# One transformer block in one launch: the shift of the attention's maximum on ScalarE, all lower parts of the probabilities on GpSimd, relative scores by one load, rotary sums out of the PSUM bank

## What is computed

```python
def _L0_attn_ref(x, w_q, w_k, w_v, w_o, rel_emb):        # 16 heads of 8 features
    q = _apply_rotary_interleave(shape(x @ w_q.T), cos, sin) / sqrt(DIM_PER_HEAD)
    k = _apply_rotary_interleave(shape(x @ w_k.T), cos, sin)
    scores = jnp.einsum('bhqd,bhkd->bhqk', q, k)
    rel = rel_emb[clip(pos_k - pos_q, -32, 32) + 32]
    scores = scores + jnp.einsum('bhqd,qkd->bhqk', q, rel)
    attn = softmax(where(causal, scores, NEG_INF))
    ctx = jnp.einsum('bhqk,bhkd->bhqd', attn, v) + jnp.einsum('bhqk,qkd->bhqd', attn, rel)
    return ctx.transpose(0, 2, 1, 3).reshape(B, L, MODEL_DIM) @ w_o.T
...
for wg, wu, wd in experts:                                # 8 experts, 128 -> 512 -> 128
    acc = acc + (silu(x @ wg) * (x @ wu)) @ wd
...
x = x + 0.5 * ffn(layernorm(x))
x = x + attn(layernorm(x))
x = x + 0.5 * ffn(layernorm(x))
```

## Time and profile before

| | before |
|---|---|
| median of 3 runs | 1345.06 us (1344.24 to 1345.31) |
| the profiled execution | 1341.76 us, of which the span from first to last instruction is 1340.0 us |
| PE busy | 1314.1 us, 98% |
| DVE busy | 1220.2 us, 91% |
| POOL busy | 1068.3 us, 80% |
| ACT busy | 1048.7 us, 78% |
| attention's first and last `scores` | 133.7 us and 1236.1 us |

### The profile page before, as it was taken

How to read it: one execution, slowest core, us unless ns; L and a number is a source line. 1 busy time by engine, 2 the same in 40 slices (tenths; PEclk the granted TensorE clock), 3 DMA queues, 4 the chain that set the end, 5 groups by cost and what they waited for, 6 DMA issues and landing times. The chain is left out here.

```text
span 1340.0 us, 28494 instructions
## 1 busy us (share of the span) xinstructions
PE 1314.1 (98%) x8334; PEld 1052.6 (79%) x8334; DVE 1220.2 (91%) x2609; ACT 1048.7 (78%) x2098; POOL 1068.3 (80%) x980
## 2 busy tenths in 40 slices
PE   8999999999999999999999999999999999999798
PEld 6888877777788777778887778777887788888586
DVE  6887989999999999999999999999999999999565
ACT  6765878888878888788888888878888888888354
POOL 6986978889787878798778878788877887878465
PEclk9999999999999999999999999999999999999899
DMA  6504799999899999999989999999999999998300
GB/s 188 162 1 132 139 183 203 185 205 206 179 201 174 196 176 182 207 183 197 188 158 221 184 189 181 173 234 170 192 183 164 226 188 178 180 193 144 60 1 8
DMA packets 719517, 225.02 MB, mean 168 GB/s; under 512 B 653441, under 2 KB 698881, under 8 KB 719361
## 3 DMA queue, kind: packets, MB, share of 16 engines
q1 hardware_dynamic: 562224, 180.84, 69.1%
q10 hardware_dynamic: 157136, 42.36, 17.5%
HBM read 60.95 MB, written 69.86 MB: 98 GB/s over the span
## 5 line engine op out<-in xcount | busy, mean ns | idle before, releaser
L1219 POOL TENSOR_TENSOR hid_lo<-hid,hid_hi 128x512 fp32r<-128x512 f32 x512 | 663.4, 1304 | 170.9 <-ACT hid_hi L927 125.9
L921 ACT ACTIVATE hid<-work 128x512 f32<-128x512 f32 x512 | 305.8, 602 | 112.7 <-PE work L788 96.0
L1053 DVE SCALAR_TENSOR_TENSOR hid<-hid,work 128x512 f32<-128x512 f32 x512 | 343.1, 678 | 46.3 <-ACT hid L921 45.8
L1059 DVE TENSOR_TENSOR hid<-hid,work 128x512 f32<-128x512 f32 x512 | 345.6, 679 | 24.1 <-PE work L727 21.7
L927 ACT CAST hid_hi<-hid 128x512 fp32r<-128x512 f32 x512 | 318.8, 627 | 60.5 <-DVE hid L1059 36.7
L1234 POOL TENSOR_TENSOR probs<-exps,probs 128x512 f16<-128x512 f32 (+1 forms) x288 | 305.1, 1064 | 65.7 <-ACT probs L979 64.0
L968 ACT ACTIVATE exps<-work,negmax_shifted 128x512 f32<-128x512 f32 (+2 forms) x320 | 188.4, 605 | 46.0 <-DVE negmax_shifted L1159 27.3
L1153 DVE TENSOR_REDUCE negmax<-work 128x1 f32<-128x384 f32 (+3 forms) x352 | 219.9, 631 | 0.9
L784 PE MATMUL work<-xt,wg 128*128 128x512 f32 x512 | 205.6, 402 | 4.0 <-DVE hid L1053 2.5
L725 PE MATMUL work<-xt,wu 128*128 128x512 f32 x512 | 204.5, 399 | 0.5 <-ACT g_s L955 0.2
L808 PE MATMUL acc<-hid_lo,wd 128*128 128x512 f32 x512 | 203.4, 400 | 1.1 <-POOL hid_lo L1219 0.9
(11 more groups left out here) (94 smaller groups left out, 1745.6 us busy)
## 6 DMA issues: line engine op xcount, KB each, us to landing
prob_window_scratch<-probs SPq DMA_DIRECT2D x384, 80.0 KB, 2.9
rel_win<-rel_window_scratch ACTq DMA_DIRECT2D x250, 96.0 KB, 3.6
q_scratch<-rope SPq DMA_DIRECT2D x16, 512.0 KB, 4.6
qq<-q_scratch ACTq DMA_DIRECT2D x32, 256.0 KB, 3.5
k_scratch<-rope SPq DMA_DIRECT2D x16, 512.0 KB, 4.2
rel_window_scratch<-g_s SPq DMA_DIRECT2D x32, 256.0 KB, 3.8
k_pad<-k_scratch SPq DMA_DIRECT2D x128, 64.0 KB, 3.6
prob_window_scratch<-probs SPq DMA_DIRECT2D x32, 256.0 KB, 3.8
```

The lines of the kernel that those rows point to most:

```text
L921: act.activation(hid[:, arg % HB, :], work[bank_of["gate", arg]][:, :], ACT.Tanh, scale=0.5).then_inc(s_tanh, 1)
L1053: dve.scalar_tensor_tensor(out=hid[:, arg % HB, :], in0=hid[:, arg % HB, :], scalar=1.0, in1=work[bank_of["gate", arg]][:, :], op0=ALU.add ...
L1059: dve.tensor_tensor(hid[:, arg % HB, :], hid[:, arg % HB, :], work[bank_of["up", arg]][:, :], ALU.mult).then_inc(s_hid, 1)
L1219: pool.tensor_tensor(hid_lo[:, arg % HH, :], hid[:, arg % HB, :], hid_hi[:, arg % HH, :].bitcast(F32), ALU.subtract).then_inc(s_hlo, 1)
```

## The change

- `lent` is gone: all 352 tasks put their exponentials into `exps` (two buffers), all lower parts are made by POOL, and the bank of a task is free after `exp`. DVE makes no lower part of probabilities.
- `shift` is one ACT instruction for a task (1, 2 or 4 columns), with the bias in a small constant tile; DVE makes none. 
- `load_window` is one DMA of 128 rows by 160 columns (320 KB) where it was two of 64 rows by 96 columns (96 KB each), on ACT's queue.
- The product with the sines goes back into the PSUM bank it came from, and the sum reads it there.
- `ln_scaled` signals each of its four tiles, and PE transposes each as it comes.
- At the very end, the last `lo` (chunk 511) is DVE's, and `acc`, `sum_turned`, `sum` and `store` of the last pass are done in two halves.
- The planner's costs follow, and every number of `LATER` is another, and so is the whole order.

```diff
-    LATER = {"acc": -1001.3, "attention_sum": -224.3, "band_turn": -664.1, "band_values": -890.3, "constants":
...
+    LATER = {"acc": -1204.3, "attention_sum": 8.3, "band_turn": -791.5, "band_values": -878.0, "constants":
...
-        step("POOL", 1.25, at + 3.7, "lo", n, ("hi", n), ("down_lo", back(n, HH)))
+        step("POOL" if n < NP * CH - 1 else "DVE", 1.25 if n < NP * CH - 1 else wide(L), at + 3.7, "lo", n, ("hi", n), ("down_lo", back(n, HH)))
...
-            step("DVE", wide(L) + w % 2 * 0.9, at, "rotate", (t, w), ("project", (t, w)))
+            step("DVE", wide(L) * (1 + w % 2), at, "rotate", (t, w), ("project", (t, w)))
...
-                step("ACT", 1.03, max(begin - 13, first - 13), "load_window", quad, ("qrel_store", gg),
+                step("ACT", 0.42, max(begin - 13, first - 13), "load_window", quad, ("qrel_store", gg),
...
-                 ("load_k", quad // NT), done_with(back(k, 2)))
+                 ("load_k", quad // NT), ("exp", back(k, 2)))
-            if lent(k):
-                step("DVE", 0.07 * HEADS[i], due[k] + 0.8, "shift", k, ("largest", k))
-            step("ACT", HEADS[i] * 0.07 + columns / 1200, due[k] + 1, "exp", k, ("shift" if lent(k) else "largest", k),
-                 ("p_lent", lent_before(k, EB) if lent(k) else None))
-            step("ACT", act_wide(columns) + 0.04 * lent(k), due[k] + 1.5, "p_hi", k, ("exp", k), ("store_band", back(k, PB)),
+            step("ACT", 0.15, due[k] + 0.8, "shift", k, ("largest", k))
+            step("ACT", HEADS[i] * 0.07 + columns / 1200, due[k] + 1, "exp", k, ("shift", k), ("p_lo", back(k, EB)))
+            step("ACT", act_wide(columns) + 0.04, due[k] + 1.5, "p_hi", k, ("exp", k), ("store_band", back(k, PB)),
                  ("p_turn", back(k, PB)))
-            if lent(k):
-                step("POOL", 0.04 + columns / 475, due[k] + 2, "p_lent", k, ("p_hi", k))
-            else:
-                step("DVE", wide(columns), due[k] + 2, "p_lo", k, ("p_hi", k))
+            step("POOL", 0.04 + columns / 475, due[k] + 2, "p_lo", k, ("p_hi", k))
...
+    spare = next(b for b in range(BANKS) if tenant[b][0] in ("gate", "up"))
...
-                    sp.wait_ge(s_sum, PASS_OF["B", arg] + 1)
-                    sp.dma_start(out_v[arg], x_s[arg % XB][:, :].rearrange("p (t d) -> p t d", t=NT)
-                                 ).then_inc(s_out[arg % XB], 16)
+                    x = x_s[arg % XB][:, :].rearrange("p (t d) -> p t d", t=NT)
+                    halves = (slice(0, NT),) if arg < B - 1 else (slice(0, NT // 2), slice(NT // 2, NT))
+                    for h, half in enumerate(halves):
+                        sp.wait_ge(s_sum, PASS_OF["B", arg] + 1 + h)
+                        sp.dma_start(out_v[arg][:, half, :], x[:, half, :]).then_inc(s_out[arg % XB], 16)
...
+            def norm_turned(m, bank):
+                for i in range(NT):
+                    pe.wait_ge(s_xn, NT * m + i + 1)
+                    done = pe.transpose(bank[:, i * P:(i + 1) * P], xn[:, i * P:(i + 1) * P], ident[:, :])
+                done.then_inc(s_xnt, 1)
...
-                    if was == "scores" and not lent(x):
-                        pe.wait_ge(*lower_part(x))
-                    if was == "scores" and lent(x):
+                    if was == "scores":
                         quad, i, places, _ = task(x)
                         pe.wait_ge(s_exp, unit(quad, places[-1]) + 1)
...
-                    pe.wait_ge(s_acc, arg + 1)
-                    transposes(bank, acc_t).then_inc(s_ftok, 1)
+                    if arg < NP - 1:
+                        pe.wait_ge(s_acc, arg + 1)
+                        transposes(bank, acc_t).then_inc(s_ftok, 1)
+                    else:
+                        pe.wait_ge(s_hid, NP * CH)
+                        for i in range(NT):
+                            half = (bank, work[spare])[i // 2]
+                            if i % 2 == 0:
+                                pe.wait_ge(s_acc, arg + 1 + i // 2)
+                            done = pe.transpose(half[:, i * P:(i + 1) * P], acc_t[:, i * P:(i + 1) * P], ident[:, :])
+                            if i % 2 == 1:
+                                done.then_inc(s_ftok, 1)
...
-                    act.mul(acc_t[:, :], acc[:, :], 0.25).then_inc(s_acc, 1)
+                    if arg < NP - 1:
+                        act.mul(acc_t[:, :], acc[:, :], 0.25).then_inc(s_acc, 1)
+                    else:
+                        for half in (slice(0, L // 2), slice(L // 2, L)):
+                            act.mul(acc_t[:, half], acc[:, half], 0.25).then_inc(s_acc, 1)
...
+                if name == "shift":
+                    quad, i, places, keys = task(arg)
+                    place = unit(quad, places[0]) % (2 * NQ)
+                    act.wait_ge(s_max, arg + 1)
+                    act.activation(shifted[:, place:place + len(places)], negmax[:, place:place + len(places)],
+                                   ACT.Identity, scale=1.0, bias=log_scale[:, 0:1]).then_inc(s_shifted, 1)
...
-                    halves = ((0, P, 0, W),) if arg < WB else ((0, P // 2, 0, P // 2 + R), (P // 2, P, P // 2, W))
-                    for top, end, left, right in halves:
-                        act.dma_start(rel_win[top:end, arg % WB, left:right, :].rearrange("p c a -> p (c a)"),
-                                      bass.AP(zwin_t, gg % 2 * NQ * TILE + i * HQ * W + top * NQ * W + left * HQ,
-                                              [[NQ * W, end - top], [1, (right - left) * HQ]])
-                                      ).then_inc(s_win[arg % WB], 16)
+                    act.dma_start(rel_win[:, arg % WB, :, :].rearrange("p c a -> p (c a)"),
+                                  bass.AP(zwin_t, gg % 2 * NQ * TILE + i * HQ * W, [[NQ * W, P], [1, HQ * W]])
+                                  ).then_inc(s_win[arg % WB], 16)
...
+                if name == "lo" and arg == NP * CH - 1:
+                    dve.wait_ge(s_hhi, arg + 1)
+                    dve.wait_ge(s_dlo, arg + 1 - HH)
+                    dve.tensor_tensor(hid_lo[:, arg % HH, :], hid[:, arg % HB, :],
+                                      hid_hi[:, arg % HH, :].bitcast(F32), ALU.subtract).then_inc(s_hlo_last, 1)
                 if name == "sum":
                     kind, t = PASSES[arg]
                     x = x_s[t % XB]
-                    dve.wait_ge(s_ftok, arg + 1)
-                    dve.tensor_tensor(x[:, :], work[bank_of["sum_turned", arg]][:, :], x[:, :],
-                                      ALU.add).then_inc(s_sum, 1)
+                    halves = (slice(0, L),) if arg < NP - 1 else (slice(0, L // 2), slice(L // 2, L))
+                    for h, half in enumerate(halves):
+                        dve.wait_ge(s_ftok, arg + 1 + h)
+                        bank = work[(bank_of["sum_turned", arg], spare)[h]]
+                        dve.tensor_tensor(x[:, half], bank[:, half], x[:, half], ALU.add).then_inc(s_sum, 1)
...
-                    dve.scalar_tensor_tensor(out=rope[:, (LO, HI)[w % 2], :], in0=work[bank_of["project", arg]][:, :],
+                    bank = work[bank_of["project", arg]]
+                    dve.scalar_tensor_tensor(out=(a, bank[:, :])[w % 2], in0=bank[:, :],
                                              scalar=(QSCALE, 1.0)[w // 2], in1=(cos_s, sin_s)[w % 2][:, :],
                                              op0=ALU.mult, op1=ALU.mult).then_inc(s_rope, 1)
                     if w % 2 == 1:
                         dve.wait_ge(s_rope, rotated(t, w))
                     if w == 1:
-                        dve.tensor_tensor(a, a, b, ALU.add).then_inc(s_rope, 1)
+                        dve.tensor_tensor(a, bank[:, :], a, ALU.add).then_inc(s_rope, 1)
                     if w == 3:
 
-                        dve.scalar_tensor_tensor(out=a, in0=a, scalar=rel_k0[:, 0:1], in1=b,
+                        dve.scalar_tensor_tensor(out=a, in0=a, scalar=rel_k0[:, 0:1], in1=bank[:, :],
                                                  op0=ALU.add, op1=ALU.add).then_inc(s_rope, 1)
...
-                if name == "shift":
-                    quad, i, places, keys = task(arg)
-                    place = unit(quad, places[0]) % (2 * NQ)
-                    dve.wait_ge(s_max, arg + 1)
-                    for n in range(len(places)):
-                        done = dve.tensor_scalar(shifted[:, place + n:place + n + 1], negmax[:, place + n:place + n + 1],
-                                                 math.log(SCALE), None, ALU.add)
-                    done.then_inc(s_shifted, 1)
-                if name == "p_lo":
-                    quad, i, places, keys = task(arg)
-                    cols = len(places) * keys
-                    dve.wait_ge(s_phi, arg + 1)
-                    dve.scalar_tensor_tensor(out=probs[:, arg % PB, cols:2 * cols],
-                                             in0=exp_of(arg)[:, 0:cols], scalar=SCALE,
```

(6 more changed lines are left out.)

102 lines of the change are left out of this document (40 added, 62 removed).

## The result

The changed kernel is **slower**: 1357.15 us (median of 4 runs, 1356.34 to 1357.78) against 1344.65 us of the kernel before in the same session (1343.33 to 1345.31), a ratio of 1.0086 with a 95% interval from 1.0065 to 1.0106. The forecast was 1331.8 us, in a range from 1322 to 1342. The profiled execution has a span of 1354.6 us where before's was 1340.0. (That execution of the kernel before, 1341.76 us in all, is faster than each of its later ones, 1343.01 us and up, so differences between spans and between medians can disagree by some 3 us.)

A forecast was written before the change was run, and what follows sets the result against it. PE, busy 98%, was taken to set attention's pace, with the large loss before the last pass. Gains of 9.25, 1.9, 0.6, 1.0 and 0.5, middle net 0, sum to 13.25: 1345.06 becomes 1331.8 us, range 1322 to 1342.

The forecast's parts named there:

- the middle: Attention with fewer matmuls beside it: DVE, ACT and POOL shares of 89/93/91% called bearable, net 0.
- Cost 0: One window load on ACT's queue: 16 MB more, 0 to 6.8% more time, hidden by buffers loaded ahead, cost 0.
- The hole: PE's idle interval before the last pass, 11.5 us, shrinks to its 2.25 us of work: gain 9.25 us.
- The slow clock: Eleven matmuls behind the hole take 2.50 us instead of 4.40, as the clock need not fall: gain 1.9 us.
- the end: Last lower part on DVE and last pass finished in halves: gain 1.0 us, from 0.3 to 1.5.
- The first norm: Kernel start: PE transposes the first layer norm's tiles as they come, gain 0.6 us.
- The shift: Shift of the maxima on ACT in attention: 0.25 us for each of 352, 88 us in all.
- The rotary sums: DVE's sums of 1338 ns for q and k become about 683 ns with an operand in the bank, some 10 us.
- no ceiling at 1.01: The middle's DMA share of 1.01 is no limit, since one 20 us stretch had 1.20 with PE fully busy.
- Rival 2: Attention can't run tighter; two `exps` buffers and POOL's queue move the hole into the middle: 1354 us, chance 0.08.
- rival 3: Same loss at a third of a microsecond a group, or slower transfers: 1342.5 to 1347.8 us, chance 0.07.

The follow-up runs named there:

- before_one_load: The kernel before, order kept, with each window loaded by one DMA of 320 KB instead of two of 96 KB: 1354.92 us, ratio 1.0066 to the kernel before.
- experiment 6: Changed kernel, plain copies for its DMA transposes, one load of 96 of 160 window columns (192 KB), needed columns left out: 1326.83 us, ratio 0.9838 to the kernel before.
- after_two_loads: The changed kernel, order kept, with each window loaded by two DMAs of 96 KB as before: 1369.61 us, ratio 1.0162 to the kernel before.
- after_block_copies_two_loads: The changed kernel with plain copies for its DMA transposes and each window loaded by two DMAs of 96 KB: 1361.77 us, ratio 1.0115 to the kernel before.
- after_block_copies_shift_vector: The changed kernel with plain copies for its DMA transposes and the shift of the maxima back on DVE: 1346.00 us, ratio 0.9983 to the kernel before.

## Why the prediction was wrong, point by point

**The step that failed** is the middle, "net 0", together with "Cost 0" for the one load: both left out what DMA transfers cost. The sum needed attention 24.6 us shorter, and it became 3.9 us longer. With the transposes replaced by copies the same order is 23 us faster, and with 96 columns for a window as well attention takes 1075.9 us, near the 1078 that were wanted. The points one by one:

**The hole: right.** Expected 9.25 us. From the last `scores` to `gate` 480 PE has 95 matmuls more, 21.6 us of work, and needs 11.9 us more, so 9.7 are gained. **The slow clock and the end: right.** Together 2.9 expected, 2.8 measured (2.6, with one matmul more in the stretch); DVE's last lower part took 0.73 us (0.68 to 1.34 expected):

```profile
1348.80 0.73 DVE L1081 TENSOR_TENSOR hid_lo<-hid,hid_hi 128x512 fp32r<-128x512 f32 x1 [0.69 <-ACT hid_hi L910]
```

**The first norm:** 0.9 us where 0.6 were expected. The longer stay at the slow clock, for which part of the 0.75 us had been taken off, didn't come: of the matmuls that follow each other every 0.43 us PE has ten before (from 10.86 us on) and seven after (from 10.57).

**The shift: too low, and it didn't matter.** 0.25 us was taken, 0.296 to 0.317 came, 103.8 us in all and not 88. The Trainium skill's figure (ScalarE: Activation LUTs, "What ACT_TABLE_LOAD costs"), 280 ns, was nearer. **The rotary sums: 691 and 748 ns**, 683 expected.

**One load, "cost 0": wrong.** This is the first step that failed. The bound was right (0 to 6.8% of DMA time; the queue's time rose by 21.9% x 1360.9 - 17.5% x 1340.0 = 63.5 us, or 4.7% of the span, in `before_one_load`). The choice of its lower end was not: the argument for it was one stretch of 20 us with a share of 1.20 and PE busy throughout. That shows that a loaded DMA was survived in that stretch; it shows nothing of the tail. Its price is 9 us in the old order and 6 to 10 in the new one without transposes.

**The middle, "net 0": wrong by 28.5 us, in its reason more than its arithmetic.** The shares of DVE, ACT and POOL were compared and found bearable, and experiment 6 shows that they are: ACT and POOL at 89 and 88% and attention in 1075.9 us. What was looked at and set aside ("no ceiling at 1.01") is the fourth resource, the DMA engines, at a share of 1.01. A tighter attention leads to the same transfers in less time and puts each nearer to the one who needs it. Of the 25 us between the forecast and the median (1331.8 and 1357.15), the copies give back 23 by the ratios. Not all of it belongs to this change, since the copies help the old order as well (by 9 us). Nor had the prediction a price for what a wait of PE does to the clock in the middle (6.8 us at most here).

**Rival 2 had the place and the sign, at a chance of 8%, by another mechanism.** Attention was not run tighter and the hole's gain was lost in the middle. But its mechanism, two `exps` buffers and POOL's queue, is only a link: `exp` waits 9.5 us for POOL's part in all, and in the traces with copies, where these buffers are the same, it waits 8.4 and the loss is gone. The round that PE's waits lead back to is that of the four `probs` buffers with the transpose in it. Slower transfers stood in rival 3, at 7%, but with a loss of about half the size. What would show the forecast wrong was told rightly (more than 15 us of idle time, PE waiting for `exps`), "and these for POOL" wasn't.

**Open.** No run has the changed kernel with windows of 96 columns, a fifth `probs` buffer or the shift on DVE and its transposes in place, so how the 23 us split between the transposes as such and the added bytes behind them isn't shown. That the bytes made them late is shown in the old order; in the new one only ACT's wait in `after_two_loads` (2.8 us for 15.0) speaks for it, and there ACT was held by its issues as well. No run has the shift on ACT or all lower parts on GpSimd alone in the old order, so what these two are worth by themselves is open. Nor was an order measured whose planner counts what the transfers take.

## What to carry to other kernels

Before an order is made tighter, put the DMA engines into the list of the engines whose share is compared, and look at the longest landings of the transfers on the path, not at their median: in this kernel the medians of good and bad are 3.9 and 4.0 us, the longest 7.7 and 11.0. And when one larger DMA replaces two smaller ones, weigh both sides: the issues that it saves on the queue of a compute engine (125 issues were worth 35 us in an order planned without them), and the bytes that it adds (16 MB cost 6 to 10 us). The run with one issue and the smaller number of bytes was the fastest of all, but it leaves out columns that the kernel needs; whether a right one can have both isn't shown.

## What the runs showed of the hardware

- The packets of a transpose by DMA take longer than those of a copy of the same bytes: SP's queue took 897 us of 16 engines' time with transposes and 756 with copies in the new order, and 926 and 760 in the old one, for 180.8 MB each time. These times can overlap on an engine, since the share reaches 1.20.
- An issue of a DMA on ACT usually takes 0.33 us (one load of 320 KB) or 0.62 us (96 KB of 64 rows), but now and then up to 4.4 us (changed kernel) and 5.85 us (`after_two_loads`), and ACT's list stands meanwhile. Ten of the 253 in `after_block_copies_two_loads` took over 1.5 us. The larger DMA was the quicker one to issue.
- Four waits of PE of 2.0 to 3.5 us in the changed kernel's attention came with a fall of the granted clock to 1.2 GHz (0.87 on the mean of each stretch of 13 us); two other waits of 2.0 and 2.1 us (at 406 and 772 us) came with none.
- A shift of the maxima on DVE beside GpSimd took 144 ns for one column and 501 and 565 ns on the mean for two and four (`after_block_copies_shift_vector`); on ACT it took 297, 317 and 296 ns.
- The packet's length counts in DMA time, but less than in proportion: 39% more bytes on ACT's queue (42.36 to 58.73 MB) in hardly fewer packets took 27% more time (234.5 to 298.0 us, before against `before_one_load`).
